# Joining the selective-scan stage and the attention stage of a four-stage kernel into one block, with the scan's tail interleaved with the first attention steps

## The reference, cut to what matters

```python
x = x + _L1_attn_ref(_layernorm(x), ...)     # the scan stage
x = x + _L1_ffn_ref(_layernorm(x), ...)      # the attention stage

# scan stage
x0 = _rmsnorm(x, rms1_w)
x1 = _mamba(x0, ...)                          # 16 states; gate by silu(z); out_proj
x = x1 + x
x2 = _rmsnorm(x, rms2_w)
x3 = _mlp(x2, ...)                            # relu, relu, linear
return x + x3

# attention stage, one of two layers
h = shift_token(x)
q, k, v = split(h @ wqkv)                     # 8 heads of 64
q, k = rotary_xpos(l2norm(q) * qs, l2norm(k) * ksc)
x = x + local_attention(q, k, v) @ wo         # windows of 64
h = layernorm(shift_token(x)) * lg + lb
a, g = split(h @ w1 + b1)
x = x + (a * gelu(g)) @ w2 + b2
```

## Time and profile before

| what | value |
|---|---|
| median of 3 runs | 1678.2 us (1675.26 to 1679.69) |
| time of the profiled execution | 1673.4 us |
| its span, first to last instruction | 1671.6 us |
| mean granted TensorE clock | 0.929 of full speed |
| busy: PE, DVE, ACT, POOL | 1368.5, 1240.6, 1086.1, 927.7 us |

### The profile page before, as it was taken

How to read it: one execution, slowest core, us unless ns; L and a number is a source line. 1 busy time by engine, 2 the same in 40 slices (tenths; PEclk the granted TensorE clock), 3 DMA queues, 4 the chain that set the end, 5 groups by cost and what they waited for, 6 DMA issues and landing times. The chain is left out here.

```text
span 1671.6 us, 23460 instructions
## 1 busy us (share of the span) xinstructions
PE 1368.5 (82%) x8131; PEld 734.8 (44%) x8150; DVE 1240.6 (74%) x1782; ACT 1086.1 (65%) x1847; POOL 927.7 (55%) x484
## 2 busy tenths in 40 slices
PE   6748068667767888888888668999999999999987
PEld 2216067522223333333333335555555555555553
DVE  2974145338689989999989189888888888888863
ACT  4423045278856666666666258888888888888874
POOL 0440624300598888788888057555555556666641
PEclk9867589888789999999999789999999999999999
DMA  1005421210000000003000011111111111121110
GB/s 65 1 0 95 132 58 53 75 48 0 3 1 0 1 1 1 0 1 133 0 1 0 15 39 32 46 27 45 27 45 27 45 27 46 33 52 33 39 26 26
DMA packets 49001, 54.21 MB, mean 32 GB/s; under 512 B 10434, under 2 KB 32116, under 8 KB 48500
## 3 DMA queue, kind: packets, MB, share of 16 engines
q1 hardware_dynamic: 46580, 47.98, 11.6%
q0 software_dynamic: 2304, 4.74, 0.9%
HBM read 20.15 MB, written 9.47 MB: 18 GB/s over the span
## 5 line engine op out<-in xcount | busy, mean ns | idle before, releaser
L1153 POOL TENSOR_TENSOR ssm_dbu<-ssm_dtu,ssm_b_all 128x1024 f32<-128x1024 f32 x128 | 299.5, 2362 | 43.6 <-ACT ssm_b_all L1077 43.4
L1782 POOL TENSOR_TENSOR at_direct<-at_direct,home_dt 128x1024 f32<-128x1024 f32 x64 | 152.3, 2380 | 287.1 <-DVE home_dt L1872 287.1
L940 PE MATMUL ssm_bank<-ssm_seen,ident 128*128 128x512 f32 x512 | 249.6, 611 | 40.0 <-POOL ssm_seen L1162 37.8
L1071 ACT ACTIVATE ssm_bank<-home_dt,ssm_decay 128x512 f32<-128x512 f32 x256 | 173.2, 691 | 60.7 <-DVE ssm_state L1255 59.3
L1255 DVE TENSOR_TENSOR_SCAN ssm_state<-ssm_bank,ssm_dbu 128x512 f32<-128x512 f32 x128 | 149.0, 1208 | 20.1 <-POOL ssm_dbu L1153 13.3
L1255 DVE TENSOR_TENSOR_SCAN ssm_state<-ssm_bank,ssm_carry,ssm_dbu 128x512 f32<-128x512 f32 x128 | 156.3, 1266 | 7.3 <-ACT ssm_bank L1071 4.6
L940 PEld LDWEIGHTS ssm_bank<-ssm_seen,ident 128*128 128x128 f32 x512 | 96.8, 194 | 126.5 <-issue 67.2
L1077 ACT ACTIVATE ssm_b_all<-ssm_bank 128x512 f32<-128x512 f32 x128 | 75.8, 592 | 103.1 <-PE ssm_bank L917 79.6
L1565 PE MATMUL at_two<-home_u,at_hs 128*128 128x512 f32 x256 | 129.2, 628 | 9.6 <-ACT at_kT L1712 5.6
L1787 POOL TENSOR_TENSOR home_u<-home_u,at_inv 128x1024 f32<-128x1024 f32 x64 | 121.5, 1898 | 18.6 <-DVE at_inv L1883 18.6
L1793 POOL TENSOR_TENSOR at_direct<-at_direct,at_rnorm 128x1024 f32<-128x1024 f32 x64 | 123.1, 1924 | 0.2
(11 more groups left out here) (237 smaller groups left out, 3318.0 us busy)
## 6 DMA issues: line engine op xcount, KB each, us to landing
at_v_mix<-at_v SPq DMA_DIRECT2D x112, 128.0 KB, 2.4
at_hs<-branch SPq DMA_DIRECT2D x64, 128.0 KB, 2.3
moe_w<-in_moe_w SPq DMA_DIRECT2D x16, 256.0 KB
moe_to_experts<-moe_empty SPq DMA_DIRECT2D x10, 258.0 KB, 7.9
moe_slot_rows<-moe_to_experts SPq DMA_DIRECT2D x10, 258.0 KB, 2.9
x<-in_x SPq DMA_DIRECT2D x8, 256.0 KB, 3.5
moe_rows<-moe_from_experts SPq DMA_DIRECT2D x8, 256.0 KB, 4.8
home_dt<-in_turn SPq DMA_DIRECT2D x2, 1024.0 KB
```

Source lines behind the costliest of these rows:

```text
L940: last = nc.tensor.matmul(bank[Y0 + half][:], ident[:], seen[:, n % 2, half], start=False, stop=n == STATES - 1)
L1071: nc.scalar.activation(bank[DA0 + half][:], chunk_of(dt[:, half], t), ACT.Exp, scale=decay[:, half, n:n + 1]).then_inc(r[f"da{half}"], 1)
L1153: nc.gpsimd.tensor_tensor(dbu[:, i % RING], dtu[:, t % 2], b_all[:, i % 2:i % 2 + 1, :].broadcast_to([P, 2, CH]), ALU.mult).then_inc(r["db ...
L1782: nc.gpsimd.tensor_tensor(direct[:, n % TURNED], direct[:, n % TURNED], crossed[:, n % 2], ALU.add).then_inc(s["added"], 1)
```

## The change

The two stages become one block (`mamba_and_attention`), without a barrier between them. What was the loop body of the attention becomes one function per engine and step (`tensor_step(g)` and so on). They are called from inside the scan's loop over i: from i = 130 (VectorE, GpSimd) or 132 (TensorE, ScalarE) on, one attention step every third i, each written behind the tail's instructions of the same i. So steps 0 to 5 (on VectorE and GpSimd 0 to 6) stand between pieces of the tail; the rest follows in a loop. Since nothing separates the two, waits are added where a buffer or bank is taken over: on `y` (last scan step), `ready`, `variance`, `down` and `operands`. The scan's ring tensors and banks are given back before the attention's are laid out over them, while the tail's weights are kept; W0 and W1, the tail's two PSUM banks, move to 6 and 7, and q, k, squares, probabilities, their transposes and the hidden layer move to parts of `home_*` that the tail doesn't hold. `tables(1)` and `fold()` move from VectorE's step 2 to step 0. ScalarE's table load at the attention's start (L1669) is dropped. Indentation is ignored in this diff.

```diff
+OPENS, EVERY = ALL_STEPS, 3
+AHEAD, BEHIND = 2, 4
...
-def mamba(nc, mem, dram):
+def mamba_and_attention(nc, mem, dram):
...
-    B0, W0, C0, W1, Y0, DA0 = 0, 1, 2, 3, 4, 6
+    B0, C0, DA0, Y0, W0, W1 = 0, 1, 2, 4, 6, 7
...
+        ring.close()
+        attend = attention(ctx, nc, mem, dram, r)
         block = ctx.enter_context(nc.Block())
...
+        def attended(i):
+
+            g, phase = divmod(i - OPENS, EVERY)
+            return g if phase == 0 and g >= 0 else None
+
+        def attended_through(i):
+
+            return (i - OPENS) // EVERY + 1
...
-            sp.wait_ge(r["operands"], 16 * len(loads))
+            sp.wait_ge(r["operands"], OPERANDS)
+            attend.sync_program()
...
+                if i == OPENS + BEHIND:
+                    attend.tensor_start()
+                if attended(i - BEHIND) is not None:
+                    attend.tensor_step(attended(i - BEHIND))
+            for g in range(attended_through(LAST_STEP - BEHIND), LAST + 1):
+                attend.tensor_step(g)
...
+                if attended(i - BEHIND) is not None:
+                    attend.scalar_step(attended(i - BEHIND))
+            for g in range(attended_through(LAST_STEP - BEHIND), LAST + 1):
+                attend.scalar_step(g)
...
+                if attended(i - AHEAD) is not None:
+                    attend.gpsimd_step(attended(i - AHEAD))
...
+                if i == OPENS + AHEAD:
+                    attend.vector_start()
+                if attended(i - AHEAD) is not None:
+                    attend.vector_step(attended(i - AHEAD))
...
-        "qk": late("dt", 0).rearrange("p (k n) -> p k n", k=2),
-        "square": late("dt", 1).rearrange("p (k n) -> p k n", k=2),
+        "qk": [late("dt", n)[:, 0:2 * INNER] for n in range(2)],
+        "square": [late("u", n)[:, 0:2 * INNER] for n in range(2)],
...
-def ffn(nc, mem, dram):
+def attention(ctx, nc, mem, dram, r):
...
             def shift(q):
+            if q < SEQS:
+                sp.wait_ge(r["ready"], up_to(q * CHUNKS + CHUNKS - 1))
...
+        sp.wait_ge(r["y"], up_to(ALL_STEPS - 1))
             for to, name in ((eye16, "eye16"), (mask, "mask")):
...
+    def tensor_start():
+        pe.wait_ge(r["operands"], OPERANDS)
...
                     pe.wait_ge(s["gelu"], (c - 1) * PARTS_OF_HID + 1)
+        else:
+            pe.wait_ge(r["ready"], up_to(2 * SEQS - 1))
...
-            act.preload_act_table_set("natural_log_exp_and_others")
...
+            if g == 0:
+                act.wait_ge(r["ready"], up_to(2 * SEQS - 3))
...
+            if n == 0:
+                act.wait_ge(r["variance"], up_to(2 * SEQS - 1))
...
+    def vector_start():
+        dve.wait_ge(r["y"], up_to(ALL_STEPS - 1))
+        dve.wait_ge(r["operands"], OPERANDS)
             nc.vector.memset(hs[64:128, :, 0:1], 0.0).then_inc(s["edge"], 1)
             nc.vector.memset(hs2[64:128, :, 0:1], 0.0).then_inc(s["edge"], 1)
+        tables(0)
...
-                if g == 2:
+        if g == 0:
                     tables(1)
...
+            if n == 1:
+                dve.wait_ge(r["down"], up_to(2 * SEQS - 1))
...
-STAGES = [min_gru, experts, mamba, ffn]
+STAGES = [min_gru, experts, mamba_and_attention]
```

## The result

Four runs of the changed kernel took 1656.19 us in the median (1653.51 to 1658.49), runs of the kernel before on the same chip 1678.56 (1675.26 to 1679.69): a ratio of 0.9869, 95% interval 0.9849 to 0.989, or 22 us less. In a second set of runs the ratio was 0.9883 (0.9864 to 0.9902). The profiled execution took 1656.13 us and has a span of 1654.3.

The account below looks back on a forecast made before the run. Chains between 925.4 us and the filled attention pipeline, about 82 us, come ahead of TensorE's full stretch; starting step 6 27.2 us earlier at full clock, cut to 21.5 for low clock, gives 1678.2 - 21.5 = 1656.7 us, range 1650 to 1670.

Parts of the forecast that it names:

- its signs: After the change: tile 0's projection 6 to 8 us behind gate, tile 6's 54 to 65, clock 0.8 to 0.95.
- What bounds it: Passage from scan to attention: chains bound 82 us from 925.4 us on, TensorE at full clock bounds the long part.
- Step 6 as the finish line: Attention step 6, at 1007.79 us before: what it gains, the end gains, as long as TensorE stays full.
- Rival (d): Steps 6 to 10: a TensorE wait, above all for `ready`, takes the lead back; 1678 us, chance 0.06.
- The walk at full clock: Gate to step 6, link by link at full clock: tile 6 at 980.6 instead of 1007.79, 27.2 us earlier.
- the 12 one-column products: TensorE, ahead of tile 0's projection: 24 weight loads at 0.195 us each, priced at 4.69 us.
- Shifted copies hidden: SyncE's four copies for tile 0, 4.15 us, end at 931.4, hidden by 1.8 us behind TensorE's work to 933.2.
- Tables and fold ahead of `branch`: VectorE, chunk 7's tail: tables 2.36 us twice, then 2.8 to 936.2; delays the tail by 8 us, shared with ScalarE's copies.
- The fold out of VectorE's full stretch: Steps 0 to 6: 7.3 us of tables and folding leave VectorE; seven steps take 47.4 us instead of 49.1.
- The barrier: Between scan and attention, 952.38 to 953.7 us: it goes, along with the idle ScalarE table load.
- The clock: Passage to step 6: each us at low level costs 0.40; gain 15.7 to 27.2 us, middle 21.5 taken.
- the likeliest case: Passage to step 6: low clock for part of the fill, gain 12 to 25 us, chance 0.60.

Follow-up runs that it names:

- e15: e4 with three more unused matmuls ahead of the output projection of the last chunk but one; step 6 at 53.53 us behind the gate.
- e3: Changed kernel with both pairs of tables and the fold behind chunk 7's branch sum instead of ahead of it; step 6 at 59.65 us behind the gate.
- e8: Kernel before with only the second tables and the fold moved from step 2 to step 0; ratio 0.9977 to the kernel before.
- e2: Changed kernel with the second tables and the fold back in step 2; step 6 at 59.66 us behind the gate.
- e13: Changed kernel with every attention step six places of the tail later; ratio 0.9914 to the kernel before.
- e4: Changed kernel with three unused matmuls, one behind the value product of step 0 and two behind that of step 1; ratio 0.984 to the kernel before.
- once more: The changed kernel run and profiled a second time, nothing changed; step 6 at 59.68 us behind the gate, end 82.50 us.
- e14: e1 with the second tables and the fold back in step 2, so of the change mainly the barrier's removal is left; ratio 0.9998 to the kernel before.
- e1: Changed kernel with only the interleaving taken out, all attention steps behind the whole tail; ratio 1.0 to the kernel before.
- e9: Kernel before with three unused matmuls in chunk 7's tail, behind the output product and the mean of squares; ratio 0.9986 to the kernel before.
- e6: Changed kernel with an attention step at every sixth place of the tail instead of every third; step 6 at 62.37 us, time that of the changed kernel.

## Why the prediction was right

**The number.** 1656.7 predicted, 1656.19 measured. By its parts it is less exact: the gain at step 6 was 22.7 (predicted 21.5), and the profile's own account is 22.7 - 3.5 in the end - 1.9 of scatter ahead of the gate = 17.3 = 1671.6 - 1654.3. The prediction had neither of the last two; its time agrees with the medians because the profiled execution of before was 4.8 us under its median and that of after was at it. That it agrees to half a microsecond is luck: 5.4 us that it left out, against 4.8 of that difference and 1.2 by which the gain at step 6 was larger. Of its signs, the projection of tile 0 came earlier than the 6 to 8 us that it had (5.70); that of tile 6 (59.66), the four tables and the clock of the fill (0.89) are as it says.

**What bounds it: right.** Step 6 as the finish line holds: the lead there, 22.7 us, is 22.7 at step 63 too (667.25 - 644.51), and TensorE waits nowhere for `ready`. Rival (d) is out.

**The walk at full clock: right to 1 us but for one term.** Against the only fill that ran at full clock throughout, with its three added matmuls, it had steps 0 to 6 at 7.8, 13.5, 21.5, 29.5, 37.1, 45.1 and 55.2 us behind the start of the gate; e15 has 5.70, 11.69, 19.78, 27.71, 35.53, 43.89 and 53.53. Each is 1.2 to 2.1 less. The term is the 12 one-column products (24 rows), for which I kept 4.69 us from a stretch at the low level: at the upper level they took 2.45.

**Shifted copies hidden: right, by less.** The projection began at 5.70, where I had 7.8. The last copy is issued at 930.63; if it takes the 2.30 us of before, it lands at 932.93, and TensorE goes from the one-column products to the projection at 933.02 without a gap. The margin of 1.8 us is gone, and which of the two ends last is not shown.

**Tables and fold ahead of `branch`: right in that it costs nothing, over-priced in itself.** I had the branch sum end 10.9 us behind the gate's end; it ended 7.4 behind it (935.97). The tables took 4.63 us for four, as priced (4.72), the fold's product 1.05 instead of 2.30. e3 takes the whole delay away and gains nothing, for the reason given then: ScalarE has tile 0 first.

**The fold out of VectorE's full stretch: right in sign.** Alone it is worth 3.1 us (e8), woven 0 (e2): in the weave VectorE is not what the passage waits for.

**The barrier: over-read.** The prediction lists it among what goes. By itself it brings nothing at step 6 (82.37), with the early fold 2.9 us there (79.50) and nothing in time. That step 0 comes 27.6 us earlier, on which its 25.5 us "at tile 0 already" rest, is the weave's. And the lead at step 0 is not the gain: e13 gives up 10.45 us of it and loses 2.9.

**The clock: right as the likeliest case, its price a little low.** Estimated 0.40 us for each at the low level, measured 0.45. The walk had 35.5 us of TensorE in 53.9; e15's passage has 45.04 in 53.53, and the same sum gives 45.04/(90.08 + 8.49) = 0.46. I took 5.7 us off, the fill lost 6.1. The 5.7 were the middle between two bounds and not worked out, so that they fit is in part luck; e15 shows that the same instructions can have 1.64 us less of it. The low level was over at about 954. The Trainium skill ("TensorE: Matmul & The Clock Gate", section on HAM oscillation) puts the drop down to long idle gaps; the trace again agrees in part: the clock fell past 933, when TensorE had last had gaps of 1.45 and 0.78 us and then 24 one-column products, and it did not fall again (1.00 from 936.45 on in e4) when three matmuls of no use were put between those of use. Why e15 kept the clock up where e4 did not, these gaps do not tell: both kernels have them.

**The end: missed.** Nothing in the prediction allows for another clock some 660 us later, where both kernels issue the same instructions. The end took 3.5 us more, and why stays open.

## What to carry to other kernels

When two phases meet, ask which engine waits in the tail of the first and put the head of the second there; taking the barrier away without that gave nothing here, for the next wait (the copies, then the clock) stood right behind it. Once they are woven, their spacing matters much less and the lead at the first step says little: read the gain where the pipeline is full. And where a chain is lean, a few matmuls of no use in its gaps can pay for themselves, provided that they don't wait for what ends the gap: three gave 4.5 us at step 6 in the new fill and 3.6 in the old tail (0.3 to 0.4% and 0.14% in time).

## What I had not expected of the hardware

- **The clock mostly repeats.** In four traces of the new order (after, once more, e2, e3) the steps of the passage agree to 0.03 us and the ends to 0.04 us, though their gates start between 924.85 and 927.32 us. But e4 and e15, with the same instructions, differ from the first microseconds behind the gate (step 1 at 13.33 and 11.69 us), so the instructions alone do not fix it. The Trainium skill ("TensorE: Matmul & The Clock Gate", on the HAM clock gate) tells that one kernel can show a different number of slow matmuls from run to run; these four traces show no such scatter behind the gate; e4 and e15 do.
- **It differs far away.** Kernels with the same 568.2 us between steps 8 and 63 and the same instructions behind them (before, e8, e14, e1, e9, e13, e6, e4 and the changed one) had ends of 78.8 to 82.8 us; the output projection in the end took 5.30 us in e4 and 6.43 in the changed kernel. In the changed kernel the clock fell a second time there, to 0.72 over 1632 to 1638 us. What it follows there is not shown: TensorE's work over those 568 us is the same.
- **VectorE and GpSimd hold each other up.** Before, two tables took 2.36 us alone and 4.49 beside a product of GpSimd (from 975.83 on, 3.26 us), and the fold's product 2.30 beside the next one, where it took 1.05 alone in the changed kernel. It is not always VectorE that loses; in e2, where two tables began just ahead of GpSimd's product, that product took 4.40 us instead of 2.35, and the fold's product behind them 4.40:

```profile
950.92 2.35 DVE L1861 TENSOR_TENSOR home_dt<-home_dt,home_z 128x1024 f32<-128x1024 f32 x2
951.08 4.40 POOL L1832 TENSOR_TENSOR at_direct<-at_direct,home_u 128x1024 f32<-128x1024 f32 x1 [3.77 <-DVE home_u L1923]
953.59 4.40 DVE L1873 TENSOR_SCALAR home_z<-home_z,ffn_ln_g 128x682 f32<-128x682 f32 x2
```
